# A graph network on one core: mixing read and counted tables in the second segment sum

## The reference, cut to what matters

```python
def sage_conv(x, edge_index, W_l, b_l, W_r, n):
    agg = jax.ops.segment_sum(x[src], dst, num_segments=n)
    return agg @ W_l.T + b_l + x @ W_r.T
h = relu(sage_conv(x, ...))
out = sage_conv(h, ...)
x = layernorm(x + out)
```

## Time and profile before

| | us |
|---|---|
| median of 3 runs | 4174.96 |
| the profiled execution's own time | 4183.78 |
| its span in the profile | 4181.9 |
| set-up, until the first gather of the first pass | 0 to 123.9, the pass itself starts at 68.9 |
| first pass | to 1062.4 |
| dense stage | to 1098.3 |
| second pass, read part | to 1637.7 |
| second pass, counted part | to 1847.9 |
| second graph layer | to 4181.9 |

### The profile page before, as it was taken

One profiled execution on the slowest core, in us unless ns is written; L12 is line 12 of the kernel. 1 busy time (PEld: TensorE's weight loads), 2 busy tenths in 40 slices (PEclk: granted clock), 3 DMA queues, 4 the chain that ended last, 5 costly groups with the idle time before them and its releaser, 6 DMA issues. The chain is left out here.

```text
span 4181.9 us, 84275 instructions
## 1 busy us (share of the span) xinstructions
PE 3058.1 (73%) x26045; PEld 2368.5 (57%) x26045; DVE 2315.7 (55%) x6793; ACT 2882.7 (69%) x7743; POOL 2971.7 (71%) x2976
## 2 busy tenths in 40 slices
PE   4899999999788888985545666676657657666645
PEld 2555556666466666655444665565656656556544
DVE  7887765655211113555225558557566576575575
ACT  4888878788533335861001987988979979979867
POOL 4677777775477777735777777777777777777655
PEclk9999999999899999996555777767777777777767
DMA  3455555556699995014434555555545545545532
GB/s 85 174 202 221 214 220 214 201 201 219 252 392 370 367 369 208 14 25 111 88 84 106 135 135 137 135 138 134 139 122 152 140 120 152 135 130 141 125 91 82
DMA packets 348311, 698.23 MB, mean 167 GB/s; under 512 B 125786, under 2 KB 207892, under 8 KB 340089
## 3 DMA queue, kind: packets, MB, share of 16 engines
q1 hardware_dynamic: 257456, 621.34, 42.0%
q0 software_dynamic: 88576, 72.82, 11.1%
q10 hardware_dynamic: 1969, 0.10, 0.0%
HBM read 437.98 MB, written 255.99 MB: 166 GB/s over the span
## 5 line engine op out<-in xcount | busy, mean ns | idle before, releaser
L1850 POOL DMA_INDIRECT gath<-fs_scratch,src_idx x1568 | 1553.2, 991 | 486.3 <-issue 473.6
L1969 ACT ACTIVATE scratch<-scratch,bias,weight 128x32 f32<-128x32 f32 x2608 | 930.5, 399 | 38.9 <-DVE bias L2038 38.9
L856 ACT ACTIVATE scratch<-sum_x_ps_c 128x600 bf16<-128x600 f32 (+7 forms) x1003 | 775.9, 826 | 172.1 <-PE sum_x_ps_c L872 161.3
L783 POOL DMA_INDIRECT gath<-in_x,src_idx x624 | 676.4, 1084 | 283.9 <-issue 187.3
L1886 PE MATMUL ps_e<-gath,ident 128*128 128x264 f32 x784 | 323.9, 552 | 550.2 <-DMA gath<-fs_scratch,src_idx 550.2
L783 POOL DMA_INDIRECT gath<-y_scratch,src_idx x544 | 532.9, 980 | 179.2 <-issue 163.2
L1906 PE MATMUL ps_m<-scratch 128*64 128x128 f32 x3136 | 556.3, 352 | 65.1 <-POOL scratch L1873 46.6
L1949 ACT ACTIVATE scratch<-iota,dst_rel 128x128 f32<-128x128 f32 x1568 | 477.4, 387 | 166.3 <-PE ps_m L1906 159.4
L1892 PEld LDWEIGHTS ps_e<-fdw,scratch 128*128 128x128 f32 x3136 | 539.4, 259 | 64.8 <-issue 27.5
L2049 DVE SCALAR_TENSOR_TENSOR scratch<-ps_e,attn_sb 128x128 f32<-128x128 f32 x784 | 191.0, 286 | 670.4 <-PE ps_e L1892 668.1
L1906 PEld LDWEIGHTS ps_m<-scratch 128*64 128x64 f32 x3136 | 496.5, 183 | 92.0 <-issue 66.7
(11 more groups left out here) (296 smaller groups left out, 4208.9 us busy)
## 6 DMA issues: line engine op xcount, KB each, us to landing
count_scratch<-scratch SPq DMA_DIRECT2D x58, 3200.0 KB
scratch<-count_scratch SPq DMA_DIRECT2D x232, 800.0 KB
en_scratch<-gath SPq DMA_DIRECT2D x196, 264.0 KB
scratch<-en_scratch SPq DMA_DIRECT2D x196, 264.0 KB
onehot<-rel_scratch SPq DMA_DIRECT2D x198, 256.0 KB
scratch<-in_edge_attr_2x SPq DMA_DIRECT2D x390, 128.0 KB
gath<-fs_scratch,src_idx POOLq DMA_INDIRECT x1568
fdw<-fd_scratch SPq DMA_DIRECT2D x392, 33.0 KB
```

The lines of the kernel that those rows point to most:

```text
L783: pool.indirect_dma_start(out=gath[:, s, t, 0:F], out_offset=None, in_=table_dram, in_offset=bass.IndirectOffsetOnAxis(ap=src_idx[:, g, k: ...
L856: act.activation(to, ps_c[u % 3][:, :, 0:q].rearrange("p h (d a) -> p h a d", d=d), ACT.Copy).then_inc(kept, 1)
L1850: pool.indirect_dma_start(out=gath[:, s, t, :], out_offset=None, in_=fs_dram, in_offset=bass.IndirectOffsetOnAxis(ap=src_idx[:, g, k:k + 1 ...
L1969: e = act.activation(rows, rows, ACT.Exp, bias=bias[:, q, i:i + 1], scale=weight[:, q, i:i + 1], accum_out=total[:, q, i:i + 1] if i < K * ...
```

## The change

FIRST_TILES falls from 912 to 840. The first pass counts 50 blocks (859 units) and gathers 91 slots, 4 of them ahead. The second pass reads 50 blocks, counts 22 (184 tiles, 368 units) and gathers the same 68 slots.

The second pass no longer has all read blocks first. `Plan.mixed` lays out 400 steps, 8 for each read block (12 or 13 slices a step), and a last one. The units of a counted block are spread over 16 or 24 of them, and its product stands whole in one step. The read blocks have one table buffer and the counted ones the other. ps_c has two pairs there in place of three, the third serves as second accumulator of products. All 68 one-hots of that pass come from ScalarE, between its copies. In a step TensorE takes the product first, then the unit, then windows and gathered tiles. The first pass keeps its form, with other places of its 25 groups of transposes. In it the first slot's last tile now stands at step 46, the last slot's first at step 848 of 859, in the second pass the last slot's tiles at steps 398 to 400, of them five or six tiles behind the product of the last counted block.

```diff
-FIRST_TILES = 912
+FIRST_TILES = 840
...
+SHARES = 2 * QUARTERS
...
+    def mixed(self, head, blocks):
+
+        own = blocks - self.read
+        self.weight = [66.0 * ALL_HIGHS / SHARES] * (SHARES * self.read) + [0.0]
+        begin, c = 0, 0
+        for r in range(self.read + 1):
+            step = r * SHARES
+            if c < own and (c + 1) * self.read <= r * own:
+                b = self.read + c
+                first, end = head.blocks[b]["first"], head.blocks[b]["end"]
+                for u in range(first, end):
+                    at = begin + (u - first) * (step - 1 - begin) // (end - first)
+                    self.units_at.setdefault(at, []).append(u)
+                    self.weight[at] += self.cost(head, u)
+                self.products.setdefault(step, []).append((b, 0, 1))
+                self.weight[step] += 66.0 * ALL_HIGHS
+                self.order.append(b)
+                self.ends(b, step + 1)
+                begin, c = step, c + 1
+            if r < self.read:
+                for i in range(SHARES):
+                    self.products.setdefault(step + i, []).append((r, i, SHARES))
+                self.order.append(r)
+                self.ends(r, step + SHARES)
...
-        TURN, APART = 150, 32
+        TURN, APART = 100, 30
...
-            lent = sum(1 for step in range(QUARTERS * read) for i, t in taken.get(step, ()) if t == 0)
+            lent, pairs = (slots, 2) if read else (0, 3)
...
-                            if b >= 2 and i == QUARTERS - 1:
-                                sp.wait_ge(multiplied, b - 1)
-                            elif b >= 2:
-                                sp.wait_ge(quarter_used, (b - 2) * (QUARTERS - 1) + i + 1)
+                            if b and i == QUARTERS - 1:
+                                sp.wait_ge(multiplied, plan.place[b - 1] + 1)
+                            elif b:
+                                sp.wait_ge(quarter_used, (b - 1) * (QUARTERS - 1) + i + 1)
                             rows = slice(NK * i // QUARTERS, NK * (i + 1) // QUARTERS)
-                            sp.dma_start(counts[:, b % 2, rows, :].rearrange("p a q -> p (a q)"),
+                            sp.dma_start(counts[:, 0, rows, :].rearrange("p a q -> p (a q)"),
...
+                        for u in plan.units_at.get(step, ()):
+                            keep(u - plan.first_unit)
+                        for i, t in taken.get(step, ()):
+                            if t == 0 and i + 1 < lent:
+                                lend_onehot(i + 1)
...
-                            if u >= 3:
-                                pe.wait_ge(kept, u - 2)
-                            elif read and u == 1:
-                                pe.wait_ge(summed_up, read // 2 * 2)
+                            if u >= pairs:
+                                pe.wait_ge(kept, u - pairs + 1)
...
+                                if read and j >= 2:
+                                    pe.wait_ge(summed_up, j - 1)
...
+                            if b < read and i % 2 == 0:
+                                pe.wait_ge(loaded[i // 2], b * 16 + 16)
```

More of the change, by code:

```diff
@@ L122, in __init__, with counted @@
         self.end_item = head.units[self.end_unit - 1]["banks"][1][0] + 1
[L123 to L133, removed]
+        self.order, self.products, self.parts_at, self.window_at, self.add_at, self.units_at = [], {}, {}, {}, {}, {}
+        if read:
+            self.mixed(head, blocks)
+        else:
+            self.counted(head, blocks)
+        self.place = {b: j for j, b in enumerate(self.order)}
+        self.steps = len(self.weight) + 8
+        self.made_by, units = [], 0
+        for step in range(self.steps + LEAD):
+            units += len(self.units_at.get(step, ()))
+            self.made_by.append(units)
+    def counted(self, head, blocks):
+        self.order = list(range(blocks))
+        self.weight = [self.cost(head, u) for u in range(self.end_unit)]
+        self.units_at = {u: [u] for u in range(self.end_unit)}
+        for b in range(blocks):
+            after = head.blocks[b]["end"]
             if b + 1 < blocks:
@@ L140, in __init__, with cost, buffer @@
             self.ends(b, after + length + 1)
-        for step in range(QUARTERS * read, len(self.weight)):
+        for step in range(len(self.weight)):
             for _, _, length in self.products.get(step, ()):
                 self.weight[step] += 66.0 * ALL_HIGHS / length
-        self.steps = len(self.weight) + 8
+    def mixed(self, head, blocks):
[21 more added lines that the diff above has]
+                self.ends(r, step + SHARES)
+        assert c == own
+    def cost(self, head, u):
+        return 2 * (head.units[u]["size"] / 2.4 + 20.0)
+    def buffer(self, b):
+        return b % 2 if not self.read else int(b >= self.read)
     def ends(self, b, after):
@@ L856, in _, with count @@
-                        act.activation(to, ps_c[u % 3][:, :, 0:q].rearrange("p h (d a) -> p h a d", d=d),
-                                       ACT.Copy).then_inc(kept, 1)
+                        for u in plan.units_at.get(step, ()):
[3 more added lines that the diff above has]
+                                lend_onehot(i + 1)
                 @block.tensor
                 def _(pe):
[L861 to L864, removed]
+                    def count(step):
+                        for at in plan.units_at.get(step, ()):
+                            unit, u = head.units[at], at - plan.first_unit
@@ L873, in _ @@
                                               cells[:, item % RING, at:at + q], start=True, stop=True)
                             m.then_inc(counted, 1)
+                    for step in range(plan.steps):
+                        if store:
+                            count(step)
                         c, odd = divmod(step - TURN + 2, APART)
```

106 lines of the change are left out of this document (57 added, 49 removed).

## The result

The changed kernel takes 4187.26 us in the median of 7 runs (4182.75 to 4208.03), the kernel before 4174.96 (4171.11 to 4179.74): ratio 1.0039, 95% interval 1.0023 to 1.0054.

What follows compares the result with a forecast made beforehand. The prediction took POOL's gathers to bound both passes: +19.5 us in the first and -33 in the second, -13.4 us in all, so 4162 us against 4175.0, 0.3% faster, range 4138 to 4206.

Steps and rivals of the forecast that it cites:

- What bounds the kernel now: Whole kernel: POOL holds the second pass's read part, not its counted part (46 us without gathers); first pass nearly full.
- First pass, the gathers: First pass: 696 gathers at 1.259 us from 114, plus 70 us of excess, so the last ends at 1060.
- The upper bound of 96: First pass: gather excess if it grows with the number of gathers; the pass would then end at 1108.
- First pass, what stands behind the last gather: First pass end: landing 4.6 us, 10 units 8.9 us, then 8 us to the end at 1082.
- +19.5: First pass: forecast to become 19.5 us longer, ending at 1082 against 1062.4.
- I take POOL as the limit: Second pass: POOL at 10.35 us a slot sets the length, TensorE level at 10.4; called close.
- -33: Second pass: forecast 33 us shorter, 717 against 749.6: 704 us of gathers and 13 behind the last.
- The reading of the tables: Second pass: with one buffer, each quarter's 2.2 us load hides in 10.6 us; DMA share falls to about 0.6.
- The rival: Second pass: units wait for ScalarE's one-hots; 1.5 us lost a slot adds 44 us, total 4206; chance 0.22.
- The page: Gathers beside VectorE's writes: the skill page says fully blocked; the prediction read a tenth, 9.5 us, from the trace.
- the rival's 160 us: Second pass: every write of cells stops gathers fully, 160 us in place of 16, total 4306; chance 0.03.
- The sum: Whole kernel: +19.5 in the first pass and -33 in the second give -13.4 us, 4162 us.

Runs made afterwards that it cites:

- the second trace: The changed kernel run once more, unedited, for another profile, since its profiled execution was its slowest time: 4195.19 us beside 4182.97 of the kernel before.
- the first trace: The profiled execution of the changed kernel, slowest of its seven times: 4208.03 us.
- the long runs: Ten of 17 runs in which every kernel, edited or not, took a third longer: the kernel before 5503 to 5652 us in place of 4169 to 4183.

## Why the prediction was wrong, step by step

**What bounds the kernel now** was right: the read part held by POOL, the counted part not, the first pass nearly full on POOL.

**First pass, the gathers: right in time, and in part by luck.** Forecast: start 114, last gather 1060, excess 70. Measured: 112.9, 1062.5 and 73. The 100 us that the other engines save are worth nothing, as stated, and TensorE waits for rows. But the excess was put down to the writes of cells alone. Of the 73 us, 64 gathers that end 0.80 to 0.86 us after a one-hot of VectorE hold 35, and 52 that end so after a write of cells hold 8; 43 lengthened ones, 22 us, follow neither in this way. The change takes 72 such writes from this pass and gives it 9 one-hots more, so the step from 80 to 70 was reasoned from the smaller part. The upper bound of 96 doesn't follow either: 80 x 696/624 is 89.

**First pass, what stands behind the last gather: too small.** Forecast 22 us, measured 29.4, and 25.9 in the second trace. The landing was taken from the read part, 4.6 us; here TensorE begins the last slot at 1073.22, 10.7 us behind its last gather (8.3 in the second trace). Then 8 units take 10.3 us up to the last pair, where 8 x 0.885 = 7.1 would do: the clock is down for the first 6 us. The sum had ten units there, 8.9 us, though the last two are the pair with which its 8 us to the end begin. PE's timeline and the windows around it:

```profile
1073.22 0.61 PE L977 MATMUL sum_x_ps_s<-onehot,gath 128*32 128x128 f32 x2 [5.74 <-DMA gath<-in_x,src_idx]
...
1083.48 0.74 PE L924 MATMUL sum_x_ps_c<-e_tab,scratch 128*128 128x325 bf16 x4
```

```profile
1067.50:1073.20 5.70, 0.00 (x0) 0.01 (x1) 2.13 (x7) 0.56 (x1) 0.00 (x0) 0.90 0.60 88
1073.20:1079.20 6.00, 5.98 (x40) 3.53 (x40) 0.72 (x2) 2.57 (x4) 0.00 (x0) 0.53 0.01 3
1079.20:1083.50 4.30, 4.30 (x46) 2.66 (x45) 0.00 (x0) 3.40 (x5) 0.00 (x0) 1.00 0.00 0
```

So +19.5 was +29.5 in the first trace and +24.3 in the second.

**Second pass: the failed step is "I take POOL as the limit".** The working had TensorE at 9.5 us of work and 0.9 us of loss a slot, 10.4 against POOL's 10.35, and then chose POOL. The work was sized well: TensorE is busy 646.11/68 = 9.5 us a slot. The loss was the term that was too small. It came from the counted part of the kernel before, where VectorE makes the one-hots and there are three PSUM pairs; here the waits for ScalarE's copies alone are 61.4 + 6.7 + 6.3 = 74 us, 1.1 a slot. TensorE's pace is 10.61 us a slot (10.54 in the second trace, 10.50 with half the gathers). POOL's own is below the forecast: with the short one-hots its gathers take 698 us, 10.3 a slot. So TensorE is the slower by some 0.3 us a slot, and that times 68 is the 20 us by which this pass missed. Until the last gather little of it shows. By slot 21 TensorE begins a slot 23 us after its last gather, and slot 67 21 us after, and POOL, which may run up to three slots ahead, waits 18.6 us for sums in all. Then the lag stands in the open: 30.5 us behind the last gather where 13 were summed up, and 710.8 for the gathers where 704 were. -33 became -8 (first trace), -13 (second), -15 with half the gathers. Where the waits for copies are gone, the sum comes out: 13.0 us behind the last gather with short one-hots and 14.4 in the mixed order at 912, and 711.1 us of pass in both, 717 forecast.

**The reading of the tables** stayed hidden, as forecast: TensorE waits 3.1 us for them. The DMA share was forecast at 0.6 and is 0.73.

**The rival** of TensorE and ScalarE had the right mechanism, down to the unit two steps on and the 3.6 us, and the right condition, 10.55 us a slot. Its sign came too: POOL waits for sums 18.6 and 13.2 us in the two traces, 7.7 in the second pass before. It was given 0.22 and priced at 1.5 us of loss; 1.1 was enough. It should have been the forecast's equal. The main sentence against it, that ScalarE catches up while TensorE waits for rows, needs TensorE to wait, which at this pace it doesn't.

**The page.** The excess beside cells was a tenth of VectorE's writes in the sum; in the second pass it is 532.3 - 544 x 0.955 = 13 us in all where 19 were taken. Part of the 9.5 us of the row before came from the one-hots that VectorE made in that stretch. From the tenth the prediction concluded that the trace does not agree with the size of the rule, and by the single gathers (the one-hots moved to VectorE, above) this was a wrong reading. The full blocking of the Trainium skill's page "SBUF — State Buffer", section "Who interferes with whom", is what they show: a gather caught by a write of cells or by a one-hot ends 0.83 us after the end of that instruction. The tenth comes from how seldom and how late in the write a gather is caught, and the rival's 160 us supposed that each write stops a gather for its full length, which no row shows. The same section says that an instruction with two SBUF inputs disturbs only GpSimd instructions that read SBUF; the one-hot of VectorE is such an instruction, a gather reads its row numbers from `src_idx`, and the trace agrees that the two disturb each other.

**The sum.** +29.5 in the first pass, -0.7 in the dense stage, -8.3 in the second pass and +3.8 in the second layer are +24.3 between the first traces of the two kernels. With the second trace it is +24.3 - 1.0 - 13.0 + 1.2, about +11, near the 12.3 us between the medians. The forecast was -13.4: 5 to 10 us of the miss lie in the first pass, 20 to 25 in the second. The second layer differs by 8 us between two executions of the kernel before, so its share says nothing.

## What to carry to other kernels

When two engines come out within a few percent of each other, don't sum up for one of them: price both, with the wait that each may add. The slower one adds its lag at the end, and a queue that runs ahead hides it until then. Before work is moved from one kind to another, ask which engine each kind loads in the stage that receives it; here a "counted" tile cost nothing in the first pass, its replacement cost a saturated GpSimd 1.1 us, and in the second pass the moved tiles loaded the engines that were about to become the limit. Long instructions for a distant need (a one-hot for the next slot) should not be queued in front of short ones that a neighbour waits for now. And before a mean (a tenth of the write time) is carried to another mix, look at single instructions: here they show a full stop that few gathers meet.

## What the runs showed of the hardware that was not expected

A gather is stopped by VectorE for the rest of VectorE's instruction, and only if that instruction is running some 0.14 us after the gather's start: 99 of 108 lengthened gathers of the run with one-hots on VectorE end 0.80 to 0.86 us after such an instruction.

TensorE, where it waited for rows, began a slot 2 to 6 us after its last gather in the second passes of the kernel before and of the mixed order at 912 (DMA share 0.98 in the read part of the first, 0.84 in the second), and mostly 6 to 9 us in the first pass of the changed kernel, whose share is lower, 0.48. For that pass's last slot it was 10.7 us in the first trace and 8.3 in the second, 12.3, 11.8 and 12.4 with half the gathers, with one-hots on VectorE and with short ones. In the first trace a store of a 3.2 MB table, issued at 1043 to 1060 us, was under way then (3.28 MB on the store's queue from 1060 to 1075 us). No run took the stores away, so that they are the cause is not shown.

After a wait of 5.7 us TensorE's granted clock was 0.53, near its lower level of 1.2 GHz, for the next 6 us and 1.00 (2.4 GHz) behind them; a unit took 0.52 us in place of 0.30.

In the long runs (numbers of the changed kernel's, 5620 us in its trace) a gather takes the same time (525.69/544 = 0.966 us), but the mean clock is 0.73 and ScalarE waits 326.5 us in the second pass for something that the profile calls remote. What slows them was not found; one and the same chip gave runs of both lengths. There the mixed order at 912 loses 0.5% where it gains 0.85% otherwise.
